# Causal attention: clearing the future part of diagonal probability tiles on VectorE in place of mask products on TensorE

## The reference

```python
q = _layernorm(q, gq, bq)
k = _layernorm(k, gk, bk)
scores = jnp.einsum('nhld,nhmd->nhlm', q, k) * SM_SCALE
causal = jnp.tril(jnp.ones((L, L), dtype=bool))
scores = jnp.where(causal, scores, -1e30)
attn = jax.nn.softmax(scores, axis=-1)
out = jnp.einsum('nhlm,nhmd->nhld', attn, v)
```

## Time and profile before

| | |
|---|---|
| Median of 3 runs | 4165.74 us (4160.04 to 4166.01) |
| The profiled execution's own time | 4157.98 us |
| Its span, first to last instruction | 4156.2 us |
| Mean granted TensorE clock | 0.912 of full speed |
| First attention with its steady units | about 101.7 to 965 us of the span |
| A unit without extras | 52.7 us (448.5 to 501.2 us) |

### The profile page before, as it was taken

How to read it: one execution, slowest core, us unless ns; L and a number is a source line. 1 busy time by engine, 2 the same in 40 slices (tenths; PEclk the granted TensorE clock), 3 DMA queues, 4 the chain that set the end, 5 groups by cost and what they waited for, 6 DMA issues and landing times. The chain is left out here.

```text
span 4156.2 us, 55566 instructions
## 1 busy us (share of the span) xinstructions
PE 3557.9 (86%) x21924; PEld 2566.7 (62%) x21924; DVE 2526.1 (61%) x3838; ACT 2219.6 (53%) x2873; POOL 994.3 (24%) x922
## 2 busy tenths in 40 slices
PE   4788888887999999996767777777775999999998
PEld 3445444445888889996323333333322888889998
DVE  4555555553443345554999999999897443335564
ACT  2454545554332234442888898899886332224443
POOL 3321223210002201113463262362320002210121
PEclk7999999998999999998787878888777999999999
DMA  3000000001001103432000000000001001012332
GB/s 116 1 1 1 1 1 1 1 1 61 6 20 37 33 33 111 105 87 73 1 1 1 1 1 1 1 1 1 1 1 61 6 6 40 28 47 79 95 90 54
DMA packets 86804, 124.91 MB, mean 30 GB/s; under 512 B 7767, under 2 KB 73257, under 8 KB 86544
## 3 DMA queue, kind: packets, MB, share of 16 engines
q1 hardware_dynamic: 68880, 100.18, 7.1%
q0 software_dynamic: 17664, 21.17, 3.1%
HBM read 85.15 MB, written 42.55 MB: 31 GB/s over the span
## 5 line engine op out<-in xcount | busy, mean ns | idle before, releaser
L487 DVE TENSOR_REDUCE a_mxp<-a_deep 128x1 f32<-128x512 f32 (+3 forms) x768 | 392.0, 552 | 348.4 <-PE a_deep L667 289.5
L1817 DVE TENSOR_TENSOR b_w<-b_w 128x2048 f32<-128x2048 f32 x256 | 582.5, 2307 | 22.9 <-ACT b_w L1895 14.7
L1854 ACT ACTIVATE b_w<-b_ring 128x1024 f32<-128x1024 f32 x512 | 480.7, 1053 | 85.5 <-PE b_ring L1937 85.0
L1925 PE MATMUL b_acc<-b_w,b_vg 128*32 128x512 f32 x2048 | 348.0, 762 | 157.3 <-DVE b_w L1817 157.2
L1895 ACT ACTIVATE b_w<-b_w 128x2048 f32<-128x2048 f32 x256 | 468.0, 1898 | 1.4
L1367 ACT ACTIVATE f1hid<-f1ring 128x512 f32<-128x512 f32 (+2 forms) x256 | 132.6, 518 | 577.6 <-PE f1ring L1447 560.6
L1367 ACT ACTIVATE f2hid<-f2ring 128x512 f32<-128x512 f32 (+2 forms) x256 | 132.6, 518 | 576.7 <-PE f2ring L1447 559.4
L586 ACT ACTIVATE a_prob<-a_wide 128x1024 f32<-128x1024 f32 (+1 forms) x320 | 294.1, 943 | 235.9 <-PE a_wide L697 162.2
L1285 DVE TENSOR_TENSOR f1hid<-f1hid,f1ring 128x512 f32<-128x512 f32 (+2 forms) x256 | 150.2, 587 | 440.2 <-ACT f1hid L1367 440.1
L1285 DVE TENSOR_TENSOR f2hid<-f2hid,f2ring 128x512 f32<-128x512 f32 (+2 forms) x256 | 150.2, 587 | 439.5 <-ACT f2hid L1367 439.4
L1937 PE MATMUL b_ring<-b_qT,b_kT 64*128 64x512 f32 x1024 | 258.6, 552 | 132.8 <-ACT b_w L1854 96.5
(11 more groups left out here) (340 smaller groups left out, 6940.1 us busy)
## 6 DMA issues: line engine op xcount, KB each, us to landing
X<-expert_in SPq DMA_DIRECT2D x16, 650.0 KB, 5.0
expert_in<-a_zeros SPq DMA_DIRECT2D x8, 650.0 KB, 10.8
X<-in_x SPq DMA_DIRECT2D x4, 1024.0 KB, 10.3
x_mid<-X SPq DMA_DIRECT2D x8, 512.0 KB, 3.2
f1raw_x<-in_rd SPq DMA_DIRECT2D x4, 1024.0 KB
f1raw_xf<-in_rg SPq DMA_DIRECT2D x4, 1024.0 KB, 4.9
f1raw_xf<-in_ru SPq DMA_DIRECT2D x4, 1024.0 KB, 7.0
f1raw_g<-in_rg SPq DMA_DIRECT2D x4, 1024.0 KB, 4.8
```

What stands on the lines that cost most here:

```text
L487: v.tensor_reduce(mxp[:, t, 2 * e + h, i:i + 1], dslot(step, h)[:, 0:n], AX_X, ALU.max).then_inc(s_dve, 1)
L1817: v.tensor_tensor(one(m), one(m), one(m), ALU.mult).then_inc(s_wts, 1)
L1854: s.activation(w[:, m, 2 * pair:2 * pair + 2, :].rearrange("p h n -> p (h n)"), slot(at + pair), ACT.Ln, scale=SHEP_EPS ** -2).then_inc(R. ...
L1925: last = pe.matmul(acc[32 * h:32 * h + 32, qc, :], vg[:, u % 2, h, x, :], w[:, x, h, :], start=(x == 0), stop=(x == TB - 1))
```

## The change

The mask products go. `scores` ends its group with its last product. A new step `cut(u, k)` stands in the list for each diagonal step k: behind the steps of k + 1 (for k = 11 behind all scores). VectorE does it: it waits for the exponential of all parts of step k, and takes, in place, the minimum of the first 128 columns of the four heads (128 partitions by 512 elements, f32) with a constant tile `past` that has 3e38 where the key is visible and 0 where it is not. `values` of a diagonal step waits for the cut in place of the exponential. The tile `past` is made by GpSimd at the start, before the kernel's other buffers are set. There are 8 cuts in a unit, 128 in all, and `end` in `spread` grows by 8, to 46 in a unit without extras, so that the `max` steps sit at other places of the list.

```diff
+    def diagonal(k):
+        qc, kt = STEPS[k]
+        return kt * P >= qc * QC
+    def cut(u, k):
+        return [("cut", u, k)] if diagonal(k) else []
...
             if k >= 2:
                 main += [("values", n, k - 2)]
+            if k >= 1:
+                main += cut(n, k - 1)
...
+        main += cut(n, NS - 1)
         end = len(main)
...
+        past = sb("past", [P, P])
+        s_cut = sem("a_future_cleared")
...
                 set_constants(pool, c)
+                pool.memset(past[:], 3.0e38)
+                pool.drain()
+                pool.affine_select(out=past[:], in_=past[:], compare_op=ALU.is_ge, fill=0.0, base=0,
+                                   pattern=[[1, P]], channel_multiplier=-1)
...
+                    elif what == "cut":
+                        u, k = step[1:]
+                        copied(dve, ("scores", u, k, parts(k) - 1))
+                        lo = QC - width(k)
+                        edge = prob[:, k % PROBS, :, lo:lo + P]
+                        v.tensor_tensor(edge, edge, past[:].unsqueeze(1).to_broadcast([P, HG, P]), ALU.min).then_inc(s_cut, 1)
...
-                                                 stop=not diag)
-                        if diag:
-                            for h in range(2):
-                                edge = dst[:, h * QC:(h + 1) * QC].rearrange("p (e n) -> p e n", e=pairs)[:, :, 0:P]
-                                last = pe.matmul(edge, c["identb"][:], c["mask_k"][:].unsqueeze(1).to_broadcast([P, pairs, P]),
-                                                 start=False, stop=True)
+                                                 stop=(y == pairs - 1))
...
-                        copied(pe, ("scores", u, k, parts(k) - 1))
+                        if diagonal(k):
+                            pe.wait_ge(s_cut, CUT_AT["cut", u, k] + 1)
+                        else:
+                            copied(pe, ("scores", u, k, parts(k) - 1))
```

More of the change, by code:

```diff
@@ L232, in attention_a @@
     DEEP_AT = places({"max": 2, "back": 1, "project": 1})
+    CUT_AT = places({"cut": 1})
     DEEP_USES = {"max": 2, "back": 1, "project": 1}
@@ L681, in _ @@
                         n = width(k)
-                        diag = kt * P >= qc * QC
                         pairs = PAIRS // parts(k)
```

## The result

The changed kernel takes 4248.57 us (median of 4 runs, 4244.04 to 4255.8); the kernel before, run beside it, 4165.88 us. The ratio is 1.0208, interval 1.019 to 1.0226: slower by 83 to 87 us, where 52 were forecast. The spans of the two profiled executions differ by 86.1 us (4242.3 against 4156.2). The last copy of an output tile of the first attention starts at 1052.10 us, 962.65 before: 89 us are lost there, and a little comes back behind it.

The account below looks back on a forecast made before the run. VectorE was taken to lead in stretch A, TensorE in B. 49 + 2 - 1 + 0.6 + 4 = 55 us gave 4213 on the profiled 4158, 4221 against the median; forecast 4218, range 4148 to 4252, likeliest case 4190 to 4235.

Parts of the forecast that it names:

- A and B: A, up to the peak's end, VectorE leads: +2.7 us; B, then to first stack transpose, TensorE's: +0.8 us.
- The clock: More waits of TensorE in A bring falls to half clock: two taken at 1.8 us each, 4 us, bounds 0 to 25.
- The mask products: 24 mask products leave TensorE in each of 16 units: 2.96 us a unit, 47 us in all.
- The cut at 0.65: Each of 128 cuts takes VectorE 0.65 us, 83 us in all; 0.4 us extra for cut 3 beside GpSimd's `norm`.
- The order: The new list moves query block 2's 384-column reduce pair behind `qkv.1`, into the busy stretch A: 1.02 us.
- Unit 14: Unit without `qkv`, taken as a long A: 2 us more.
- Unit 15: Unit without `max` steps: the mask time is kept, less a cut in the tail, -1 us.
- The start: The tile `past` stands before GpSimd's release of the start: +0.6 us.
- Rival 4: One more clock fall in every unit, 21 us beyond the forecast: 4239; chance 0.14.
- Rival 1: Faster: TensorE leads and cuts vanish in VectorE's idle time; at most 47 us kept, 4119, half about 4143; chance 0.18.
- Rival 3: Full price: every cut delays the chain and the masks give nothing back, 83 us: 4249; chance 0.08.
- What would show it: In unit 6: reduces nearly gapless, peak 2.6 us later, maxima waits over 120 us, cut 0.65, plain unit some 56 us.

Follow-up runs that it names:

- the idle products: The changed kernel with two TensorE products opening each part of `scores` in steps 2 to 5, overwritten by the real ones: 1.0167 of the kernel before.
- experiment 4: Neither mask products nor cuts, steps in the old order, causal mask left out, against the kernel before: ratio 1.0041 (1.0026 to 1.0055).
- experiment 7: The kernel before, mask products kept and no cuts, with `qkv` in two steps of 8 products so a row-maximum step can fall between: 0.9987.

## Why the prediction was wrong, step by step

The direction was right, and one term, the clock, was far too small. For plain units, a straight line through the lengths of units 2, 3, 6, 7, 10 and 11 against their half-clock time separates the two parts: before 51.2 us at none, changed 55.0 us at none, and 0.21 us more for each us at half clock. (Five of the changed kernel's six points lie between 20 and 27 us at half clock, so its 55.0 hangs on unit 11: with a price of 0 to 0.45 us for each us at half clock, the widest range of such lines here, unit 11 gives 56.5 to 53.4.)

- **A and B, 3.5 us a unit: right as far as can be told.** At full clock 55.0 - 51.2 = 3.8, with 2.2 to 5.3 as the widest bounds. In unit 11 the peak's last piece ends 31.2 us after the output copy that closes the unit before, 27.3 in the kernel before: 3.9, where the walk had 2.6, with one fall of the clock in it. The rest of that unit is 1.4 us longer (56.5 - 31.2 against 51.2 - 27.3), forecast 0.8, with one more fall.

```profile
807.78 0.47 PE L689 MATMUL a_deep<-a_kT,a_qT 64*128 64x128 f32 x2 [1.06 <-DVE a_mxp L506]
...
808.51 1.94 PE L732 MATMUL a_acc<-a_prob,a_vg 128*32 128x512 f32 x8
...
823.01 0.18 DVE L522 TENSOR_SCALAR a_qs<-a_neglo 128x16 fp32r<-128x16 f32 x1
```

- **The clock, 4 us with 0 to 25 as bounds: this step failed.** It counted falls, two more in all and at most one for each of 14 units, at 1.8 us. Measured are 13 more (27 against 14), within that bound, but 233 us more at half clock: a fall lasts 11.8 us in the mean where it lasted 6.1, and the one that the price was taken from, lasted 3.4. The plain units' mean is 59.4 us against 51.7: 7.7, of which 3.8 are work in line, so the other half is the clock. In the sum: 86 us measured, less the 51 of the other terms, leaves about 35 where 4 stood, 10 beyond the bound; 233 us at the line's 0.21 would be 49. The size is known no better than that, and half of it at least is argued from the lines: the idle products gave back 16 us. The error was to price the fall by the one row where a single long wait brings it and the clock soon comes back, and to take as its only cause a longer wait. Less work between the waits brings it as well: experiment 4, which adds no VectorE work and moves no step, has 108 us more of it (its waits for maxima are 86.6 us, 76.3 before).
- **The mask products, 2.96 us a unit.** The step said that their saving in A turns into waiting and that B keeps 1.5. At full clock it is 1.0 us (experiment 4's plain units: 50.2 by the line). Then the clock takes it and more: its plain units take 54.6 us in the mean, 51.7 before, and idle products in the same kernel bring them to 51.6. The prediction named this nowhere; it saw the clock as a matter of the cuts alone.
- **The cut at 0.65: 0.68, and 0.77 in the mean.** The contention was priced at 0.4 us for cut 3 alone. The longest is 1.70, and in several units two cuts, not one, lie beside `norm`.
- **The order.** It was costed inside A, as 1.02 us of a reduce moved in. By itself, with mask products, it is 1.9 us a plain unit at full clock (53.1 by the line), and another 3 by the clock. What of the 1.9 is which wait was not taken apart.
- **Unit 14, +2:** 48.9 against 40.2 us, +8.7, with 20.5 us at half clock (3.4 before). **Unit 15, -1:** 30.7 against 32.5, -1.8. **The start, +0.6:** VectorE's first instruction behind GpSimd's release begins at 13.92, 13.31 before.
- **Rival 4**, one more fall in every unit, 4239, was the right mechanism: its clock term is 25 us (4 and 21) where about 35 are left to explain, and it too had short falls. Rival 1 had TensorE's 47 us to win; experiment 4 shows that in this order there is nothing to win even with no cut. Rival 3, every cut at its full price, had 4249, and the measured median is 4248.57. That is luck: the cuts by themselves are 36 or 57 us by the order they stand in, and the order alone, which that rival prices at nothing, is 41.
- The range ended at 4252. The medians taken together stay inside it (4248.57); the ratio times the median shown before, 1.0208 x 4165.74 = 4252.4, lies just outside.
- "What would show it": the reduces in A with few gaps and the cut near 0.65 came out, and a unit at about 56 in the best case only (unit 11; the mean is 59.4). TensorE's wait for the maxima over 120 us did not (98.8, or 114 with the cuts).

## What to carry to other kernels

Before taking work off an engine that is busy for 86%, look where its idle time lies: if it waits for another engine in those stretches, the work taken off turns into more waiting there, and in this kernel also into a lower clock for TensorE's products that are left (experiment 4: 193 us at half clock, 85 before). When instructions are placed by a count over a list, leave a change's new entries out of the count, and run the order alone as a control; here it cost 41 us alone, and some 13 with the rest of the change in place, so one such control does not give its share. When a change can bring falls of the clock, ask how long each will last, and not only how many there will be. In this kernel the clearing did best on the engine that nobody waits for: the same work on GpSimd, with the row maxima given room, is what beat both kernels.

## What the runs showed of the hardware

- Idle products on TensorE made two kernels faster: 1.0208 to 1.0167 with half-clock time from 318 to 197 us, and 1.0041 to 0.9988 with 193 to 100 us. In the kernel before, where there was little to gain, they cost 0.3%.
- The clock fell behind waits of 1.14 us (with one of 0.67 ahead of it) and 1.76 us, and stayed at half for 3.4 us where TensorE never waited, for 23.9 us where it waited five times for 0.36 to 1.67 us.
- A microsecond at half clock cost 0.17 to 0.45 us of the unit's length, by the straight lines through the plain units of the kernels. That it is less than a half because part of it lies in waits for VectorE is an explanation, not tested.
- The falls come in patterns that repeat from unit to unit (experiment 7: 0 us at half clock in units 2, 6 and 10, 13.7 in units 3, 7 and 11), so that units with the same work differ by 4.5 us.
- An affine select over 128x512 f32 in SBUF takes 0.64 us on GpSimd, less than the two-input minimum on VectorE (0.68, up to 1.70 beside GpSimd's own two-input instructions).
